# Second layer of a two-layer attention and expert kernel: one ring of eight activation buffers, decays made a turn ahead, second products two units behind

## The reference

```python
# attention: a state space recurrence, N = 16 states per feature
dt = softplus(einsum('bth,gh->btg', u, W_dt) + b_dt)
A_bar = exp(dt[..., None] * A)
state = A_bar * state + dt[..., None] * B_mat * u[..., None]
y = einsum('bhn,hn->bh', state, C_mat) + D_vec * u
# feed-forward: 64 routed experts of 32 hidden, top 8, and 2 shared ones of 256
probs = softmax(xf @ router_w + router_b)
tw, ti = top_k(probs, 8); tw = tw / sum(tw)
h = silu(xf @ W1 + B1) @ W2 + B2          # for each expert e
acc = acc + cw[:, None] * h               # cw = tw where ti == e, else 0
shared = sum over 2 of silu(xf @ W1 + B1) @ W2 + B2
```

## Time and profile before

| | us |
|---|---|
| median of 3 runs (lowest, highest) | 469.74 (465.57, 470.54) |
| profiled execution, span | 473.9 |
| from 313.9 us: routed stage and end | 160 |
| TensorE busy, share of the span | 346.5, 73% |
| VectorE | 347.8, 73% |
| ScalarE | 261.5, 55% |
| GpSimd | 243.2, 51% |

### The profile page before, as it was taken

The page is one execution under the profiler, slowest core; times in us unless marked ns, Lnnn a source line. Parts: engine busy times, 40 slices in busy tenths (PEclk is TensorE's granted clock), DMA queues, the critical chain, the costliest instruction groups (busy, mean ns, idle before and its releaser), DMA issues.

```text
span 473.9 us, 5780 instructions
## 1 busy us (share of the span) xinstructions
PE 346.5 (73%) x1491; PEld 247.2 (52%) x1491; DVE 347.8 (73%) x615; ACT 261.5 (55%) x440; POOL 243.2 (51%) x254
## 2 busy tenths in 40 slices
PE   1846879667975987779506848977887887887883
PEld 0435659356854866668403524544554554554542
DVE  5679998897864866648169759908688688688674
ACT  1477654546458346374505675355856856856820
POOL 3475300704763676776800049005577877877850
PEclk9977675959997898998956975997999999999997
DMA  6374100100111112120160000004658658668574
GB/s 175 94 200 128 25 1 1 45 11 24 46 39 29 34 41 81 43 42 21 35 190 0 0 0 2 0 0 89 126 101 161 123 116 163 122 119 162 112 152 111
DMA packets 36213, 35.09 MB, mean 74 GB/s; under 512 B 12166, under 2 KB 30839, under 8 KB 36183
## 3 DMA queue, kind: packets, MB, share of 16 engines
q0 software_dynamic: 7104, 21.90, 22.7%
q1 hardware_dynamic: 29078, 12.84, 10.2%
HBM read 13.29 MB, written 4.65 MB: 38 GB/s over the span
## 4 chain that ended last, share of the span: by engine, by line
PE 35%; POOL 19%; DVE 19%; issue 13%; ACT 6%; DMA 3%; another core or an unknown queue 2%; DVEq 1%; SPq 0%; POOLq 0%; ACTq 0%
POOL state L568 10%; PE psum L1376 5%; POOL xn_tok L572 4%; PE psum L1349 4%; POOL g_hi L581 3%; PE psum L1365 3%; PE psum L1389 3%; PE psum L1443 3%; PE psum L292 3%; PE psum L293 2%; PE psum L294 2%; PE psum L1352 2%; PE psum L1355 2%; PE psum L1338 1%
## 5 line engine op out<-in xcount | busy, mean ns | idle before, releaser
L1212 DVE TENSOR_TENSOR_SCAN state<-dec,win_t 128x1024 f32<-128x1024 f32 x32 | 73.4, 2293 | 26.5 <-ACT dec L777 26.5
L568 POOL TENSOR_SCALAR state<-state,ssm_cb 128x1024 f32<-128x1024 f32 x32 | 49.7, 1553 | 48.0 <-DVE state L1212 45.0
L812 ACT ACTIVATE sil<-psum,vec_t 128x512 f32<-128x512 f32 x64 | 43.2, 687 | 48.3 <-PE psum L294 37.7
L509 POOL DMA_INDIRECT parts<-t_out,part x39 | 41.0, 1050 | 48.3 <-ACT t_out L726 41.9
L1498 PE MATMUL psum<-hid,g_w 128*128 128x512 f32 x128 | 62.1, 599 | 0.0
L1221 DVE TENSOR_TENSOR hid<-sil,psum 128x512 f32<-128x512 f32 x64 | 41.7, 676 | 12.9 <-ACT sil L812 10.9
L497 POOL DMA_INDIRECT x_tile<-normed,token x39 | 41.3, 1059 | 13.4 <-issue 10.7
L292 PE MATMUL psum<-xn_hi,g_hi 128*128 128x512 f32 x64 | 39.7, 620 | 11.3 <-ACT sil L812 11.3
L1094 DVE TENSOR_TENSOR t_hid<-t_sil,psum 128x352 f32<-128x352 f32 x39 | 20.3, 521 | 32.3 <-ACT t_sil L710 23.5
L717 ACT ACTIVATE t_hid_t<-psum 128x384 f32<-128x384 f32 x39 | 19.2, 492 | 38.9 <-PE psum L1365 25.3
L1376 PE MATMUL psum<-w_out,t_hid_t 128*128 x234 | 37.5, 300 | 2.2 <-ACT t_out L726 1.4
(11 more groups left out here) (308 smaller groups left out, 887.6 us busy)
## 6 DMA issues: line engine op xcount, KB each, us to landing
xn_tok<-state POOLq DMA_DIRECT2D x32, 512.0 KB, 4.5
e_raw<-in_L_ffn_w SPq DMA_DIRECT2D x16, 128.0 KB, 2.2
both<-parts SPq DMA_DIRECT2D x4, 512.0 KB, 5.6
e_raw<-in_L_ffn_w SPq DMA_DIRECT2D x8, 176.0 KB, 2.6
res<-in_L_attn_x SPq DMA_DIRECT2D x4, 256.0 KB, 3.8
normed<-rows SPq DMA_DIRECT2D x1, 1024.0 KB, 5.2
g_raw<-in_L_ffn_w SPq DMA_DIRECT2D x16, 64.0 KB, 2.3
g_w<-in_L_ffn_w SPq DMA_DIRECT2D x16, 64.0 KB, 2.2
```

The costliest lines, as they stand in the source:

```text
L509: pool.indirect_dma_start(out=parts, out_offset=bass.IndirectOffsetOnAxis(ap=part[:, n:n + 1], axis=0), in_=t_out[n % ORING][:, :], in_off ...
L568: own(pool.tensor_scalar(state[k][:, :], state[k][:, :], ssm_cb[:, i * GPI + k // 2:i * GPI + k // 2 + 1], 0.0, ALU.mult, ALU.add))
L812: act.activation(sil[:, c % 2, :], ps[c % 2][:, :], ACT.Silu, bias=vec_t[:, V_B1 + c // NBLK:V_B1 + c // NBLK + 1]).then_inc(h_silu, 1)
L1212: dve.tensor_tensor_scan(state[k][:, :], dec[n % DECS][:, at_half], win_t[:, at_half], 0.0, ALU.mult, ALU.add).then_inc(scanned, 1)
```

## The change

Buffers: `hid` becomes one ring of eight for shared and routed units, `sil` one of four, and there are six decay buffers, of which two lie over the place of the low and high attention inputs and two over that of the first layer's attention. Constants `DECAYS_AT` and `SCAN_BEFORE` say before which unit a pair of decays and a scan stand; units 0 to 15 are the shared ones, 16 to 79 the routed ones.

Order: two blocks of `dt` are made ahead of the turns of the logits. ScalarE makes bias, Abs and Exp of each block at once, then Ln, before its first shared silu. The exponentials of the router weights stand before unit 6, the turns of the weights before unit 11. VectorE does block 2 of the softplus ahead of the router weights and blocks 3, 0 and 1 ahead of the splits; the mask is gone, the larger of the logarithm and a polynomial is taken, and of two blocks the polynomial is partly a Square on ScalarE. On TensorE the weights' matmul of a unit stands one unit ahead, the first product two units ahead and the second product two units behind. On GpSimd the split of a group's weights stands before the first scan behind its predecessor's last unit.

```diff
+        HRING, SRING, DECS = 8, 4, 6
+        hid = [later(f"hid_{r}", [P, TB]) for r in range(HRING)]
+        sil = [later(f"sil_{r}", [P, TB]) for r in range(SRING)]
+        WEIGHTS_AT, CW_AT, COPIES_AT = 6, 11, 12
+        DECAYS_AT = {u: (2 * i, 2 * i + 1) for i, u in enumerate((14, 22, 30, 38, 46, 53, 60, 67))}
+        SCAN_BEFORE = [SHARED, SHARED, SHARED + 2, SHARED + 4]
+        for u0 in (22, 30, 38, 46, 53, 60):
+            SCAN_BEFORE += [u0 + 3, u0 + 5, u0 + 7, u0 + 7]
+        SCAN_BEFORE = [u - SHARED for u in SCAN_BEFORE + [70, 71, 73, 75]]
...
+        OUT_BEHIND = 2
...
+            g = GPI
+            for k in range(1, NSCAN):
+                while g < NG and (g - GPI + 1) * NBLK <= SCAN_BEFORE[k]:
+                    split_next(g)
+                    g += 1
+                weigh_state(k)
+                add_state(k)
...
+                e = softplus_bufs[b][0]
+                own(act.activation(e[:, :], blk(dt_t, b), ACT.Abs))
+                own(act.activation(e[:, :], e[:, :], ACT.Exp, scale=-1.0))
+                act.nop().then_inc(sp_exp, 1)
+            for b in range(POOL_LOGS, NBLK):
+                e, _, p = softplus_bufs[b]
+                act.activation(p[:, :], e[:, :], ACT.Square, scale=0.5, bias=half_mid[:, 0:1])
...
+            for u in range(SHARED + UNITS):
+                if u == WEIGHTS_AT:
                     act.wait_ge(r1_arg, 1)
                     act.activation(pair[:, :, :], pair[:, :, :], ACT.Exp).then_inc(r1_exp, 1)
+                if u == min(DECAYS_AT):
+                    act.wait_ge(win_ready, NBLK)
+                for n in DECAYS_AT.get(u, ()):
+                    decay(n)
+                if u == COPIES_AT:
                     for b in range(NBLK):
                         copy_cw(b)
+                if u < SHARED:
+                    shared_silu(u)
+                else:
+                    silu(u - SHARED)
...
+            softplus(3)
+            softplus(0)
+            softplus(1)
+            for b in range(NBLK):
+                split_cw(b)
+            dve.wait_ge(firsts_ready, 1)
+            k = 0
+            for c in range(UNITS):
+                while k < NSCAN and SCAN_BEFORE[k] == c:
+                    scan(k)
+                    k += 1
+                weigh(c)
...
+                if SHARED <= u + 1 < SHARED + UNITS:
+                    expert_weights(u + 1 - SHARED)
+                if u + 2 < SHARED:
+                    shared_in(u + 2)
+                elif u + 2 < SHARED + UNITS:
+                    expert_in(u + 2 - SHARED)
+                while done <= u - OUT_BEHIND:
+                    if done < SHARED:
+                        shared_out(done)
+                    else:
+                        expert_out(done - SHARED)
+                    done += 1
```

More of the change, by code:

```diff
@@ L148, in program @@
         both = over(base, nc.sbuf_base)("both", [P, NT, TOPK, P])
+        beside_xr = over(base, nc.sbuf_base)
         turning = over(base, nc.sbuf_base)
@@ L586, in _ @@
-            for i in range(NG // GPI):
-                group_turn(i, i == NG // GPI - 1)
+            add_state(0)
+            g = GPI
[5 more added lines that the diff above has]
+                add_state(k)
+            assert g == NG
         @block.scalar
@@ L779, in decay, with silu @@
                                scale=ssm_a[:, n:n + 1]).then_inc(decay_ready, 1)
-            for c in range(NSH * NBLK):
-                k, tb = divmod(c, NBLK)
-                if c in range(NBLK):
-                    own(act.activation(softplus_bufs[c][0][:, :], blk(dt_t, c), ACT.Abs))
-                if c == AHEAD_OF_CW:
+            def silu(c):
+                act.wait_ge(h_made, c + 1)
+                if c >= SRING:
+                    act.wait_ge(hid_done, c - SRING + 1)
+                act.activation(sil[c % SRING][:, :], ps[c % 2][:, :], ACT.Silu,
+                               bias=vec_t[:, V_B1 + c // NBLK:V_B1 + c // NBLK + 1]).then_inc(h_silu, 1)
@@ L1459, in second_biases, with expert_in, expert_weights, expert_out @@
                           skip_group_check=True).then_inc(b2_used, 1)
+            def expert_in(c):
+                g, tb = divmod(c, NBLK)
+                j = g % GPI
+                if tb == 0:
+                    pe.wait_ge(g_split, g + 1)
+                if c < 2:
+                    pe.wait_ge(cw_copied, c + 3)
+                    pe.wait_ge(cw_split, c + 3)
+                else:
+                    pe.wait_ge(h_silu, c - 1)
+                product(pe, ps[c % 2][:, :], g_hi[j][:, :], g_lo[j][:, :], blk(xn_hi, tb), blk(xn_lo, tb)
+                        ).then_inc(h_made, 1)
+            def expert_weights(c):
+                g, tb = divmod(c, NBLK)
+                if c < 2:
+                    pe.wait_ge(sh_silu, NSH * NBLK - 1 + c)
+                else:
+                    pe.wait_ge(hid_done, c - 1)
+                if c == 0:
+                    pe.wait_ge(cw_split, NBLK)
+                pe.matmul(ps[2 + c % 2][:, :], sel_now[g % GPI][:, :], blk(cw_hl, tb), start=True, stop=True
+                          ).then_inc(cwx_made, 1)
+            def expert_out(c):
+                g, tb = divmod(c, NBLK)
+                if tb == 0:
+                    pe.wait_ge(g_w2_in[g % GPI], (g // GPI) * 16 + 16)
+                pe.wait_ge(hid_done, c + 1)
+                pe.matmul(ps[4 + tb][:, :], g_w2[g % GPI][:, :], hid[c % HRING][:, :], start=False,
+                          stop=g == NG - 1, skip_group_check=True).then_inc(g_out, 1)
+            done = 0
             shared_in(0)
-            for c in range(NSH * NBLK):
-                if c == AHEAD_OF_CW:
+            shared_in(1)
+            for u in range(SHARED + UNITS):
+                if u == CW_AT:
                     turn_cw(0)
```

257 lines of the change are left out of this document (103 added, 154 removed).

## The result

| | us | ratio to before (95%) |
|---|---|---|
| before, median of 4 runs beside the change | 468.58 | |
| the change, median of 4 runs (lowest, highest) | 477.25 (475.55, 480.42) | 1.020 [1.015, 1.026] |

The change is slower by 8.7 us; 474 were forecast, slower than before but by half as much, and the range to 481 holds it. The ratios and their intervals leave out runs more than 1.5% above the fastest of their kernel: two of the four of one experiment, that with the second product ahead of the first. The profiled execution of the change is the slowest of its four (480.42 us, 3.2 above the median) and has a span of 478.7 us.

What follows compares the result with a forecast made beforehand. No engine was full; waits around ScalarE's decays lost TensorE 3.46 us a turn. Span: 313.05 + 115.9 + 7 x 3.49 = 453.3, + 15.2 (clock) + 9.85 (end) = 478.3, 4.4 slower than before: 474 us, range 462 to 481.

Steps and rivals of the forecast that it cites:

- The mechanism: Routed turns: first product u+2 needs silu u; TensorE has 2.87 us of work against 6.36, so seven waits of 3.49 us.
- None for VectorE: Sign in the routed turns: TensorE waits seven times about 3.5 us for the silu and never for VectorE.
- the two scans in a row lie in the decays' gap: Routed turns on VectorE: the two back-to-back scans, 4.6 us, fall within ScalarE's gap for decays.
- two turns seven units long: Routed stage: two turns have 7 units, last decays at unit 67 of 80; this moves waits but not their number.
- The pitch of an eight-unit turn: Routed turns: 8 x 1.78 + 3.49 = 17.7 us, the same as before, so the turns gain nothing.
- The clock term: Routed turns on TensorE: each wait lowers the clock and costs 1.9 us, for eight decay pairs 15.2 us.
- the clock holds: Rival in the routed turns: waits of 3.5 us do not lower TensorE's clock, giving 459 us, up to 464; chance 0.15.
- The front: Before the routed turns: TensorE resumes after the first decays at 313.0 in place of 323.26; net gain 5.7 us.
- The front gains nothing: Rival before the routed turns: late router exponentials, low clock through 296 to 304 us, gain shrinks to 0: 480 us; chance 0.13.
- The sum: Whole kernel: span of 478.3 us against 473.9, 4.4 us slower; 474 us forecast as run time.
- tail: End of the kernel: VectorE no longer waits for the last GpSimd transfer, 2.1 us gained; the following 9.85 us stay.
- GpSimd: Rival in the routed turns: split weights slip by 3 us, 1.5 us lost in each of 7 turns, 484 us; chance 0.10.

Runs made afterwards that it cites:

- small buffers: The change with four hidden buffers and four decay buffers in place of eight and six: 478.83 us, ratio 1.025.
- The fill: The change with the experts' weights matmul issued ten times, same result, in the seven units behind a pair of decays: 469.75 us, ratio 1.0055.
- the turns of the weights early: The change with the router weights' exponentials ahead of the first shared silu and the weights' turns and copies before units 7 and 8: 476.01 us, ratio 1.015.
- front and scans apart: The change with the router weights' exponentials ahead of the first shared silu and scans ahead of units 2, 4, 6, 8 behind the decays: 473.66 us, ratio 1.012.
- held: The change with second products held to a distance of five, those up to u-1 issued ahead of a decay unit's blocked first product: 478.07 us, ratio 1.025.
- held and front together: The change with second products held to a distance of five and the router weights' exponentials ahead of the first shared silu: 473.14 us, ratio 1.012.
- the fastest kernel: The change with router exponentials first, scans spread, second products held to distance five and SyncE's group-weight loads in order of time: 456.25 us, ratio 0.978.

## Why the prediction came out as it did

**The mechanism held.** The second products' distance makes seven waits, in first products, for the silu, of about the length worked out (3.49 us forecast, 3.48 from the starts above); buffers don't enter. The scans wait for no decay after the first. In three turns the wait was not one piece: 0.7 us for VectorE and 2.4 for the silu. "None for VectorE" failed there, and so did the reading that the two scans in a row lie in the decays' gap. Nor are two turns seven units long, but three (units 46, 53, 60 and 67 in `DECAYS_AT`). The pitch of an eight-unit turn was forecast at 17.7 us without the clock; the change has none without it (20.5 to 20.7 us), but with small buffers one turn had no half clock, and there it is 387.53 - 369.58 = 17.95 us from one waiting first product to the next.

**The clock term was a little small.** 15.2 us were charged, eight pairs at 1.9; the trace has seven at 2.5, 17.4 us. The first pair costs no clock: there TensorE waits only 1.03 us, for it arrives late. The 17.4 are those of the slowest of four executions. The fill, which does no useful work, shows that the term is real: 7.5 us back. The rival "the clock holds" is refuted for waits of 3.3 us in this kernel. By the Trainium skill's "TensorE: Matmul & The Clock Gate" (HAM oscillation) a loop with a long wait in each pass pays in each pass; in this trace it paid in seven of seven, the three of 2.4 us included. It is not so everywhere: with small buffers, and with the turns of the weights early, one of the seven waits had no half clock behind it (2.42 and 2.43 us), with front and scans apart two (3.41 and 3.31 us).

**The front was the mis-sized term.** Forecast was a net gain of 5.7 us. On the start of the second layer of the change's trace (7.1 us earlier), the steps forecast and measured, from the timelines of ScalarE, VectorE and TensorE:

```profile
278.73 1.06 ACT L850 ACTIVATE pair<-pair 128x1024 f32<-128x1024 f32 x1
...
295.29 0.60 ACT L826 ACTIVATE cw_hl<-psum 128x512 fp32r<-128x512 f32 x1 [2.88 <-PE psum L1494]
...
303.14 0.69 ACT L820 ACTIVATE hid<-psum,vec_t 128x512 f32<-128x512 f32 x1 [3.65 <-PE psum L300]
303.85 1.28 ACT L835 ACT_TABLE_LOAD   x1
```
```profile
282.62 2.49 DVE L1216 TENSOR_TENSOR xn_tok<-pair,rrow 128x1024 f32<-128x1024 f32 x2
...
298.96 0.69 DVE L1224 TENSOR_TENSOR cw_hl<-psum,cw_hl 64x512 fp32r<-64x512 f32 x1 [1.87 <-ACT cw_b L829]
```
```profile
299.62 1.91 PE L1499 MATMUL psum<-cw_b,b_sb 64*128 64x512 f32 x2
301.46 0.80 PE L298 MATMUL psum<-xn_hi,sw_hi 128*128 128x512 f32 x1
...
311.09 0.50 PE L1523 MATMUL psum<-cw_hl,sel_now 128*128 128x512 f32 x1 [1.03 <-ACT hid L820]
```

The exponentials end at 279.8 (278.6 forecast), the weights at 285.1 (284.2). The splits end at 299.65, not 296.9: each of the last two waits for a turn on TensorE and a copy on ScalarE, which I had let run beside. And TensorE had run out of work meanwhile (its shared products were done at 289.9, and in the turns it waits 0.72 and 2.00 us), and the clock was low behind that:

```profile
295.70:306.00 10.30, 10.30 (x19) 4.77 (x18) 1.39 (x2) 5.13 (x8) 0.00 (x0) 0.50 0.00 0
```

The second biases and the product before silu 13 run in there, the decays start at 303.85 in place of 298.7, and TensorE resumes at 311.09, not 305.9: 5.2 us late, which leaves 0.5 us of the 5.7. "The front gains nothing" was a rival of 0.13, with a low clock as its cause, from 296 to 304, which is 288.9 to 296.9 on this start; it came some 7 us later and lasted longer. This rival and the forecast's order of products are both what happened.

What set it off is the place of the router weights' exponentials. In all five traces that have them before unit 6 (the change, the fill, small buffers, second product first, held) the clock is at 1.2 GHz for 10.2 to 13.7 us in the turns of the weights; in all seven that have them ahead of the first shared silu it is at 2.4 GHz there, and with that edit alone TensorE resumes 60.8 us after the start of the layer, where the prediction had 59.9 and the change has 65.1.

**The sum.** Forecast was a second layer of 478.3 - 253.15 = 225.2 us; it is 232.7. The 7.5 us between are 5.2 (front) + 2.2 (clock) + 0.7 (left over in the turns) - 0.6 (tail). Against the kernel before, the 12.0 us of the traces are 17.4 (clock) less the 2.85 that before lost behind its wait of 6.2 us, less 0.5 (front) and 2.75 (tail), plus 0.7 and 0.2 in the turns. That the runs show +8.7 lies in the spread of single executions: 3.2 us by the profiled one. So the range held partly by luck: by the median run the forecast is 3.3 us short, by the traces 7.5, almost all of it in the front and the clock.

**GpSimd** was late in no turn of the change, since the waits gave it time. It is what comes next: TensorE's longest wait for its splits was 4.3 to 5.2 us in four of the experiments.

## What to carry to other kernels

When an engine's gap (here 6.5 us of decays and table loads) must be bridged, count the work that another engine has between the blocked instruction and the one before it that needed the same bank; more buffers elsewhere do not add to it, and on TensorE a bridge that is 3 us short was paid nearly twice here, 3.5 us of wait and 2.5 of clock. Saving work up for the gap only pays if what the saved work releases (here loads queued in one list on SyncE) is not needed sooner: put such a list in order of time first. Compare traces from the start of the changed stage, not from the start of the span.

## What was not expected of the hardware

VectorE's scans and GpSimd's operations hold each other up in both directions. Of the change, GpSimd's timeline and VectorE's:

```profile
412.02 2.50 POOL L502 TENSOR_SCALAR g_hi<-g_raw 128x128 fp32r<-128x128 f32 x1
```
```profile
415.87 3.02 DVE L1235 TENSOR_TENSOR_SCAN state<-dec,win_t 128x1024 f32<-128x1024 f32 x1
```

A split of 0.65 us takes 2.50 beside a scan, and a scan of 2.28 takes 3.02 beside a scaling. The Trainium skill's "SBUF — State Buffer" (Who interferes with whom) says so of VectorE with two SBUF inputs; the prediction had seen one direction only (one of the 32 scans of its trace did take 2.52 us, at 408.31, behind an average of 2.293). GpSimd's wait can outlast one scan: 4.55 us beside two in a row.

The clock fell behind waits as short as the 2.1 us of the earlier trace rows: 2.16 and 2.36 us in the fastest kernel (0.50 in the window from 391.4). Length alone does not decide it: with held and front together a wait of 2.53 us had no half clock behind it, and with front and scans apart one of 3.41 had none. A wait of up to 1.6 us by itself lowered it in no turn of any kernel here.
